# A selective-scan layer on one core: another order of the preparation over 64 scan steps, the skip term opening the sum banks, and the product with C taken one step at a time

## The reference, cut to what matters

```python
xz = hidden_states @ in_proj_w.T                 # after a layer norm; 2 x 512 channels
x, z = jnp.split(xz, 2, axis=-1)
x = silu(causal_conv4(x) + conv_b)               # 4 taps, per channel
dt, Bm, C = split(x @ x_proj_w.T)                # 16 + 16 + 16
dt = softplus(dt @ dt_proj_w.T + dt_proj_b)
def step(h, ins):                                # h: 512 channels x 16 states
    dA = jnp.exp(dt_t[:, :, None] * A)
    h = dA * h + dt_t[:, :, None] * B_t[:, None, :] * x_t[:, :, None]
    y = jnp.einsum('bdn,bn->bd', h, C_t)
y = scan(step) + x * D                           # the skip term
out = (y * silu(z)) @ out_proj_w.T               # added to the residual rows
```

## Time and profile before

| | |
|---|---|
| median of 3 runs | 2182.27 us (2181.54 to 2183.92) |
| profiled execution: its time, its span | 2181.55 us, 2179.8 us |
| granted TensorE clock, mean (1 is 2.4 GHz, 0.5 is 1.2 GHz) | 0.849 |
| first scan starts, last scan ends | 56.96 us, 613.91 us |
| busy over the span | PE 1572.5, PEld 1325.8, DVE 1119.2, ACT 912.1, POOL 930.2 us |

### The profile page before, as it was taken

The page is one execution under the profiler, slowest core; times in us unless marked ns, Lnnn a source line. Parts: engine busy times, 40 slices in busy tenths (PEclk is TensorE's granted clock), DMA queues, the critical chain, the costliest instruction groups (busy, mean ns, idle before and its releaser), DMA issues. The chain is left out here.

```text
span 2179.8 us, 28324 instructions
## 1 busy us (share of the span) xinstructions
PE 1572.5 (72%) x9844; PEld 1325.8 (61%) x9844; DVE 1119.2 (51%) x2193; ACT 912.1 (42%) x1599; POOL 930.2 (43%) x615
## 2 busy tenths in 40 slices
PE   4776866857868974863038996898692199989990
PEld 1555655657656863861027895895592088878880
DVE  6755756746767951225766345645847023222322
ACT  4775776767834442532124223744331022322220
POOL 0577576577643334651023112402005723685406
PEclk7988988988979976985558998899895599999995
DMA  3001010101011032520010001002005311333103
GB/s 110 20 21 39 20 40 20 40 20 40 20 63 28 1 117 98 187 75 23 0 47 1 1 1 42 1 11 69 1 1 210 104 63 49 126 114 109 30 20 118
DMA packets 51958, 114.44 MB, mean 53 GB/s; under 512 B 13996, under 2 KB 34377, under 8 KB 44276
## 3 DMA queue, kind: packets, MB, share of 16 engines
q1 hardware_dynamic: 43764, 75.23, 10.0%
q0 software_dynamic: 8064, 37.45, 5.1%
HBM read 87.02 MB, written 25.87 MB: 52 GB/s over the span
## 5 line engine op out<-in xcount | busy, mean ns | idle before, releaser
L839 POOL TENSOR_TENSOR HC<-H,CB 128x1024 f32<-128x1024 f32 x128 | 302.5, 2364 | 165.7 <-DVE H L739 103.7
L418 PE MATMUL ps<-ident,UT 128*128 128x128 f32 x1024 | 182.1, 307 | 58.5 <-DVE H L739 52.4
L739 DVE TENSOR_TENSOR_SCAN H<-dA,ps 128x512 f32<-128x512 f32 x128 | 154.0, 1214 | 124.6 <-PE ps L418 86.2
L418 PEld LDWEIGHTS ps<-ident,UT 128*128 128x128 f32 x1024 | 136.7, 158 | 131.0 <-DVE H L739 72.0
L570 ACT ACTIVATE UT<-DTXT,BT 128x512 f32<-128x512 f32 x256 | 181.4, 711 | 39.3 <-PE ps L418 39.2
L739 DVE TENSOR_TENSOR_SCAN H<-dA,HL,ps 128x512 f32<-128x512 f32 x128 | 160.2, 1275 | 71.7 <-PE ps L418 46.0
L580 ACT ACTIVATE dA<-DT,nA 128x512 f32<-128x512 f32 x256 | 180.8, 709 | 2.8 <-DVE DT L707 2.7
L429 PE MATMUL ps<-ident,HC 128*128 128x128 f32 x1024 | 171.5, 298 | 9.7 <-POOL HC L839 9.2
L1748 POOL TENSOR_TENSOR f_W<-f_stage,f_zeros 128x2048 fp32r<-128x2048 f32 x24 | 86.5, 3606 | 144.6 <-POOLq L1768 138.6
L429 PEld LDWEIGHTS ps<-ident,HC 128*128 128x128 f32 x1024 | 138.1, 157 | 12.5 <-POOL HC L839 10.9
L1965 DVE TENSOR_TENSOR f_XN<-f_XN,ps 128x1024 f32<-128x1024 f32 x39 | 47.6, 1221 | 173.5 <-PE ps L147 173.5
(11 more groups left out here) (490 smaller groups left out, 4306.7 us busy)
## 6 DMA issues: line engine op xcount, KB each, us to landing
f_stage<-in_f_w POOLq DMA_DIRECT2D x24, 1024.0 KB, 5.4
CB<-m_c_rows SPq DMA_DIRECT2D x16, 1024.0 KB, 4.7
f_w<-in_f_w SPq DMA_DIRECT2D x16, 1024.0 KB
f_rows_in<-f_zeros SPq DMA_DIRECT2D x13, 384.0 KB, 13.6
f_DI<-f_rows_in SPq DMA_DIRECT2D x39, 128.0 KB, 2.2
f_rows_out<-f_EO SPq DMA_DIRECT2D x39, 128.0 KB, 1.7
a_values<-a_zeros SPq DMA_DIRECT2D x8, 320.0 KB, 5.4
a_VBD<-a_values SPq DMA_DIRECT2D x8, 320.0 KB, 4.5
```

The source lines that it names most:

```text
L418: ins = pe.transpose(PS[4 + G % UR][:, t * P:(t + 1) * P], UT[:, n % 2, t, c * P:(c + 1) * P], g.ident[:, :])
L739: dve.tensor_tensor_scan(H[:, G % HR, :], dA[:, G % AR, :], PS[4 + G % UR][:, :], first, ALU.mult, ALU.add).then_inc(h_ready, 1)
L839: pool.tensor_tensor(HC[:, y:y + 2, :], H[:, s:s + 2, :], CB[:, n // 4 % CR, n % 4:n % 4 + 1, :].to_broadcast([P, 2, W]), ALU.mult).then_i ...
```

## The change

1. **Product with C.** `times_c` is called for every p instead of every second; one instruction multiplies 128x512 instead of 128x1024. In blocks 0 and 2 its small copy of the last columns (`HL`) moves to every fourth step.
2. **Skip term.** `add_skip` becomes `begin_sums` and is the first write to each sum bank (start=True on its first product), at p = 6 to 9. `sum_up` no longer opens a bank. It starts at p = 10 with three steps instead of at p = 8 with two, and has caught up at p = 14.
3. **Order of the preparation.** Every piece gets another p on all four engines: the convolution two passes per step at p = 4 to 13 instead of one at 4 to 19; `silu_x` at 14 instead of 20 (without `silu_z`); rows, B and dt at 15 to 24 instead of 23 to 31; `correct` every third step from 24 instead of every second from 30; the gated transposes at 26 to 30 instead of 8 to 13; `project_z` at 32 to 41; `silu_z` of the first half and the logarithms together at 37 instead of 20 and 40; the second half at 43 instead of 44; `add_logarithm` and `times_x` from 39 to 53 instead of 42 to 56; `transpose_dtx` at 47, 51, 55, 59 instead of 46, 50, 54, 58; `project_out` at 44 to 54 instead of 32 to 39.
4. **Banks.** `transpose_dtx` uses `PS[6]` alone and `project_out` `PS[7]` alone (before, both alternated), also before the first block and after the last. The gated transposes go 0, 1, 2, 3 over the two banks instead of 0, 2, 1, 3.

```diff
-G_ORDER = (0, 2, 1, 3)
 # PE
 def transpose_dtx(k, c):
-    out = bank(c % 2, dtxt_ready, k * CI + c + 1)
+    out = bank(0, dtxt_ready, k * CI + c + 1)
-def add_skip(k, t):
+def begin_sums(k, t):
+    if k:
+        pe.wait_ge(y_used, (k - 1) * TC + t + 1)
     for c in range(CI):
         ins = pe.matmul(PS[t][:, c * P:(c + 1) * P], XS[:, c, t * P:(t + 1) * P], skip_diag[:, c, :],
-                        start=False, stop=False, skip_group_check=True)
+                        start=(c == 0), stop=False, skip_group_check=True)
-def transpose_gated(k, i):
-    t = G_ORDER[i]
-    out = bank(t % 2, g_ready, k * TC + i + 1)
+def transpose_gated(k, t):
+    out = bank(t % 2, g_ready, k * TC + t + 1)
 # project_out
-            held[t // 2] = bank(t // 2, o_used, k * 2 + t // 2 + 1)
+            held[1] = bank(1, o_used, k * 2 + t // 2 + 1)
 # sum_up
-    if u == 0 and k:
-        pe.wait_ge(y_used, k * TC)
-                        start=(u == 0), stop=(u == NU - 1), ...
+                        start=False, stop=(u == NU - 1), ...
 # PE's loop over p
-    if 8 <= p < 11:
-        sum_up(k * NU + 2 * (p - 8))
-        sum_up(k * NU + 2 * (p - 8) + 1)
-    elif p >= 11:
+    if p == 10:
+        sum_up(k * NU)
+    if 10 <= p < 14:
+        sum_up(k * NU + 2 * p - 19)
+        sum_up(k * NU + 2 * p - 18)
+    elif p >= 14:
         sum_up(k * NU + p - LAG)
-    project_x 2..5, 10, 11, 14, 15; transpose_gated 8, 9, 12, 13; add_skip 12, 13, 18, 19
-    project_z 16, 17, 20, 21, 40..43; project_rows 23..26; transpose_b 27; project_dt 28..31
-    project_out 32..39; transpose_dtx 46, 50, 54, 58
+    project_x 2..5, 7, 8, 10, 11; begin_sums 6..9; project_rows 15..18; transpose_b 19
+    project_dt 20, 21, 23, 24; transpose_gated 26, 27, 29, 30; project_z 32..35, 38..41
+    project_out 44, 45, 46, 48, 50, 52, 53, 54; transpose_dtx 47, 51, 55, 59
 # ACT's loop
-    keep_gated 9, 10, 13, 14; silu_x and silu_z(0, 1) 20; keep_rows 27; keep_b 28
-    magnitude 29..32; logarithm 40; silu_z(2, 3) 44; keep_dtx 47, 51, 55, 59
+    silu_x 14; keep_rows 19; keep_b 20; magnitude 21, 22, 24, 25; keep_gated 27, 28, 30, 31
+    silu_z(0, 1) and logarithm 37; silu_z(2, 3) 43; keep_dtx 49, 53, 57, 59
 # DVE's loop
-    add_rows 36, 40; convolve 4..19, one pass each; add_edge 19; rectify 29..32
+    add_rows 48, 55; convolve 4, 5, 7, 8, 9, 10, 12, 13, two passes each; add_edge 13
+    rectify 21, 22, 24, 25
 # POOL
-    pool.wait_ge(h_ready, G + 2)
+    pool.wait_ge(h_ready, G + 1)
-        pool.wait_ge(hc_used, G - YR + 2)
-    pool.tensor_tensor(HC[:, y:y + 2, :], H[:, s:s + 2, :], CB[...].to_broadcast([P, 2, W]), ALU.mult).then_inc(hc_ready, 2)
+        pool.wait_ge(hc_used, G - YR + 1)
+    pool.tensor_tensor(HC[:, y, :], H[:, s, :], CB[:, n // 4 % CR, n % 4, :], ALU.mult).then_inc(hc_ready, 1)
-    for p in range(0, NU, 2):   edges 2; correct 30..36; add_logarithm 42, 46, 50, 54; times_x 44, 48, 52, 56
+    for p in range(NU):         edges 3; correct 24, 27, 30, 33; add_logarithm 39, 43, 47, 51; times_x 41, 45, 49, 53
```

More of the change, by code:

```diff
@@ L462, in _ @@
                                 project_x(k + 1, (p - 2) // 2, p % 2)
[L463 to L468, removed]
+                            if p in (7, 8):
+                                project_x(k + 1, 2, p - 7)
@@ new lines, in _ @@
+                        if k and p in (26, 27, 29, 30):
+                            transpose_gated(k - 1, (26, 27, 29, 30).index(p))
+                        if 32 <= p < 36:
+                            project_z(k, (p - 32) // 2, p % 2)
+                        if 38 <= p < 42:
+                            project_z(k, 2 + (p - 38) // 2, p % 2)
+                        if k + 1 < NK and p in (47, 51, 55, 59):
+                            transpose_dtx(k + 1, (p - 47) // 4)
+                        if k and p in (44, 45, 46, 48, 50, 52, 53, 54):
+                            i = (44, 45, 46, 48, 50, 52, 53, 54).index(p)
+                            project_out(k - 1, i // 2, i % 2)
@@ L615, in _ @@
                             keep_columns(k + 1, p - 1)
[L616 to L618 removed]
+                        if k + 1 < NK:
+                            if p == 14:
+                                for c in range(CI):
+                                    silu_x(k + 1, c)
+                            if p == 19:
+                                keep_rows(k + 1)
+                            if p == 20:
+                                keep_b(k + 1)
+                            if p in (21, 22, 24, 25):
+                                magnitude(k + 1, (21, 22, 24, 25).index(p))
+                        if k and p in (27, 28, 30, 31):
+                            keep_gated(k - 1, (27, 28, 30, 31).index(p))
+                        if p == 37:
+                            for t in range(2):
+                                silu_z(k, t)
                             if k + 1 < NK:
                                 for c in range(CI):
[L621 to L632 removed]
                                     logarithm(k + 1, c)
[L634 removed]
+                        if p == 43:
                             for t in range(2, TC):
                                 silu_z(k, t)
[L637 to L638 removed]
+                        if k + 1 < NK and p in (49, 53, 57, 59):
+                            keep_dtx(k + 1, (49, 53, 57, 59).index(p))
                 for i in range(TC):
@@ L721, in add_rows @@
                     rows = g.X[:, k * TC + 2 * j:k * TC + 2 * j + 2, :]
[L722 removed]
+                    dve.tensor_tensor(rows, rows, PS[7][:, :].rearrange("p (t d) -> p t d", t=2), ALU.add).then_inc(o_used, 1)
                 def scan(G):
@@ L848, in _ @@
                 for k in range(NK):
-                    for p in range(0, NU, 2):
+                    for p in range(NU):
                         times_c(k * NU + p)
                         if k + 1 < NK:
-                            if p == 2 and (k + 1) % KB:
+                            if p == 3 and (k + 1) % KB:
                                 edges(k + 1)
-                            if 30 <= p < 38:
-                                correct(k + 1, (p - 30) // 2)
-                            if 42 <= p < 58 and p % 4 == 2:
-                                add_logarithm(k + 1, (p - 42) // 4)
-                            if 44 <= p < 60 and p % 4 == 0:
-                                times_x(k + 1, (p - 44) // 4)
+                            if p in (24, 27, 30, 33):
+                                correct(k + 1, (p - 24) // 3)
+                            if p in (39, 43, 47, 51):
+                                add_logarithm(k + 1, (p - 39) // 4)
+                            if p in (41, 45, 49, 53):
+                                times_x(k + 1, (p - 41) // 4)
 NH, HD, SK = 16, 16, 77
```

80 lines of the change are left out of this document (27 added, 53 removed).

## The result

The changed kernel takes 2107.09 us (median of 4 runs, 2104.53 to 2108.24) against 2183.1 for the kernel before: a ratio of 0.9648, 95% interval 0.9631 to 0.9665. I had given 2114 in a range of 2080 to 2150. The profiled execution is the one of 2104.53 us, with a span of 2102.6.

What follows compares the result with a forecast made beforehand. No engine was full; some 40 us a block were waiting among PE, POOL, DVE and ACT. Blocks summed to 488.2 against 557.0, a gain of 68.8, less 0.6 outside: 2113.4, given as 2114, range 2080 to 2150.

Steps and rivals of the forecast that it cites:

- The round ends and POOL is the path from 38: Blocks 0 to 2: four-step rounds of 12.10 us become 8.85, POOL never starved from step 38; 66%.
- The price of the product: The single 128x512 product with C on POOL: 1.25 us start to start, bounds 1.18 and 1.38.
- Rival D: Slower: the single product's price cancels the gain, reaching 557 us over the blocks at 1.88 us each; 5%.
- POOL busy over 108: Sign in the windows of blocks 0 to 2: POOL busy over 108 us, with blocks of 126 to 134.
- Scan 38 behind ACT: Block 1: scan 38 starts at 79.3 us, late behind ACT by about 6, logarithms not waiting for POOL.
- The margin of `correct`: Block 1, step 37: POOL's fourth `correct` ends 1.7 us before ACT's fourth logarithm wants it.
- Rival C: ACT works so far ahead that its stops at 14 and 37 vanish; about 30 us less, 2084; 13%.
- Blocks 0 and 2: 130.8 and 131.6 us, each including 2.0 for PE's lower clock after the longer silu stop.
- The rival in the rule of the port: Denser POOL products may hold the normalisations at p = 60 to 63: some 2 us a block, 6 in all.
- Steps 0 to 14: Block 1: 5.6 us for the first scans, 25.7 for the convolution steps; last pass ends at 31.3.
- Block 3: The block without preparation: 97.6 us, summed by step, including 15.6 for steps 5 to 13.
- The tail: After the last scan: single product saves 1.1 us, bank-order transposes about 1.8, `project_out` in one bank costs 0.8; predicted -2.1.

Runs made afterwards that it cites:

- times_x_twice: The changed kernel with each `times_x` of blocks 0 to 2 made twice, one behind the other; 2119.8 us, ratio 0.9709.
- no_table_43: The changed kernel with a plain copy instead of the silu of z at step 43, so no table loads there; 2095.4 us, ratio 0.9598.
- single_old_order: The kernel before with the single product with C as its only change; 2128.0 us, ratio 0.9748.
- correct_longer: The changed kernel with the first of the three instructions of `correct` made twice, four times a block; 2111.3 us, ratio 0.9673.
- no_table_14: The changed kernel with a plain copy instead of the silu of x in blocks 1 to 3; 2091.7 us, ratio 0.9571.
- skip_after_sums: The changed kernel with the sums opening the banks at step 8 again and the skip term added at steps 9 to 12; 2110.2 us, ratio 0.9658.
- pairs_new_order: The changed kernel with the product with C in pairs of two records again; 2119.1 us, ratio 0.9703.
- start_banks: The changed kernel with the four DTX transposes before the first block alternating over two banks again; 2104.0 us, ratio 0.9630.

## Why the prediction was right, and where not

**The round ends and POOL is the path from 38.** Shown: 8.73 us a round against 8.85, 35.0 us from product 38 against 35.3; times_x_twice puts POOL's work on the path, no_table_43 takes ACT's stop at 43 off it. The explanation was too narrow: I gave the whole effect to the later `transpose_dtx`, and single_old_order shows that the single product does it alone, with an `add_logarithm` behind it in the queue. As I costed the single product by its price only (18 us of POOL's time lost), I would have foreseen no gain for it by itself.

**The price of the product.** 1277 ns against 1260 of the row it was taken from, 1.23 to 1.25 start to start. Rival D, a price above 1.88 us, is excluded. My sign "POOL busy over 108" a block did not come, 105.2 to 106.8: 64 times 0.07 on the 100.4 to 103.0 of before is 105 to 107.5, so the sign did not follow from my own price.

**Scan 38 behind ACT.** In block 1 it started at 80.2 (79.3 predicted), scan 15 to 26 took 19.9 (20.2), 26 to 32 9.3 (9.6), 32 to 38 15.2 (14.8). The margin of `correct` was 1.4 (1.7), and correct_longer shows that it is real. Rival C, in which the stops at 14 and 37 vanish in ACT's lead, did not come; no_table_14 shows that a part of a shorter stop at 14 is indeed swallowed in blocks 0 and 2, by PE.

**Blocks 0 and 2, in part luck.** For block 0 I had charged 1.5 us of waiting for the fourth `correct`; its logarithms do not wait at all. For PE's lower clock behind the longer silu stop I had added 2.0 to both; scan 15 to 26 took 20.5 and 21.1 us there against 19.9 in block 1, so 0.6 and 1.1, at a granted clock of 0.90 and 0.80 in steps 15 to 19 against 1.00. In block 2 a late start (scan 4 at 7.1; kernels with the same code have it anywhere from 5.5 to 7.7) made up for it: its 131.1 against 131.6 is closer than the terms are.

**The rival in the rule of the port.** The normalisations at p = 60 to 63 might have been held longer by the denser products, some 6 us in all. The eight of them took 5.0 us in the changed kernel and 6.3 before: this cost did not come.

**Steps 0 to 14.** Scan 15 of block 1 started at 35.8; the sum gave 31.3 + 3.4 = 34.7. Of the miss of 1.1, 0.4 is the start (scan 4 at 6.0 and not 5.6; it moves from kernel to kernel), 0.4 the steps 4 to 13 (26.1 and not 25.7) and 0.3 the stop. That PE hides behind DVE there, skip_after_sums shows.

**Block 3, the term that was mis-sized: 97.6 against 93.7.** Steps 5 to 13 took 13.9 and not 15.6; the z and output steps, which I had charged at the full 1.73 each, took 1.2 to 1.8, and steps 32 to 63 together 49.8 instead of 52.8. Steps 26 to 31 went the other way, 9.3 instead of 8.5. That the scans run on a lead of two records there is my reading of it, and no run tests it. I had charged each step its own slowest engine, which is right only where the same engine is slowest for long.

**The tail, -5.0 against -2.1.** The gated transposes in bank order were to save 1.8 and the outputs in one bank to cost 0.8. The windows from the last scan to the first output matmul, before and then after:

```profile
613.91:624.70 10.79, 6.35 (x32) 4.71 (x32) 2.49 (x5) 2.39 (x4) 2.49 (x2) 0.70 0.00 0
```

```profile
542.26:548.90 6.64, 3.91 (x26) 2.51 (x24) 2.48 (x5) 2.39 (x4) 1.76 (x2) 1.00 0.00 0
```

The granted clock there was 0.70 and is now 1.00. In the stretch of 0.70 PE had stopped for 0.95, 1.26, 0.88, 0.69 and 0.69 us between pieces of about 1 to 2 us; now its stops are 0.48, 0.57 and 0.87. The 32 output matmuls of the kernel before ran in 9.03 us, 0.28 each; the same 32 are now two rows of 3.7 for 16 each, 0.23 each. That is 1.6 us, which turns my loss of 0.8 into the gain of 0.8 that the traces show. The runs of the two halves part the 4.1 us ahead of the outputs. From the last scan's end to the first gated transpose it is 4.5 us before and 3.5 in single_old_order: 1.0 for the single product (1.1 predicted). From there to the outputs it is 6.3 before and 4.5 in pairs_new_order: 1.8 for the order of the banks (1.8 predicted). In the changed kernel it is 3.35, 1.2 less again, with the same order. The 16 transposes of pairs_new_order (granted clock 0.50) and then of the changed kernel (1.00):

```profile
557.82 3.74 PE L395 MATMUL ps<-ident,ZT 128*128 128x128 f32 x16 [0.87 <-DVE ZT L718]
```

```profile
545.61 2.57 PE L395 MATMUL ps<-ident,ZT 128*128 128x128 f32 x16 [0.87 <-DVE ZT L718]
```

So the terms of the tail were right, and what I had left out is the clock: 1.2 us ahead of the outputs and 1.6 in them. The output matmuls took 7.4 us in both kernels with the new order, and 9.0 and 9.8 in the two with the old one.

**The start, +2.8 against +2.7**, and start_banks takes most of it back.

**The rule of the port.** `add_edge` fell from 1.84 to 0.17 us; I had allowed up to 1.25. No product ran beside it: its 0.17 us is its length when nothing holds it, and this row alone bears the rule neither out nor against. In the two halves a product did run beside it. In single_old_order, block 2:

```profile
362.37 1.27 POOL L837 TENSOR_TENSOR HC<-H,CB 128x512 f32<-128x512 f32 x1
362.91 0.76 DVE L688 TENSOR_TENSOR DT<-DT,conv_edge 128x12 f32<-128x12 f32 x1
```

It ends at 363.67, 0.03 behind the product's end at 363.64. In pairs_new_order it takes 0.98 and ends 0.03 behind the end of a product of two records. That is the rule of the Trainium skill (SBUF — State Buffer, section "SBUF: two separate sides"), that a VectorE instruction with two SBUF inputs and GpSimd hold one port pair against each other for a whole instruction; the row of 1457 ns against 692 shows it at a larger size.

## What to carry to other kernels

When two in-order engines wait for each other in a ring, ask what already released work lies behind the item that the other one needs: a long instruction cut in two can break the ring as well as a new order does, even though its engine works longer. So price a split not only by its extra busy time but by what the shorter wait in front of it lets go earlier, and run each half of such a change alone before giving it the whole gain. Then move work off the engine that is now full only into steps in which the receiving engine waits for it: the same kind of move gained 8 us at steps 43 to 55 and lost 18 at steps 23 to 27.

## What the runs showed of the hardware

DVE's product of two SBUF tiles of 128x512 took 692 ns with POOL at rest and 1457 (`correct`) or 1495 (`times_x`, mean of 12) beside POOL's products; POOL's product that started while it ran took 1.72 to 1.75 us instead of 1.27. DVE's `add_edge`, 12 elements per partition, took 0.17 us with no product beside it, and 0.76, 0.98 and 1.84 us where it ended 0.03 us behind the end of one. The granted clock in blocks 0 to 3 was 0.88, 0.98, 0.94 and 1.00, where it had been 0.84, 0.87, 0.85 and 0.95. PE's 12 long stops for DTX, 69.6 us, are gone; that they are the reason is likely but not shown. I had not put this into the sum. No run prices it over the blocks; behind the last scan, 16 transposes took 3.74 us at a granted clock of 0.50 and 2.57 at 1.00.
